# One four-byte inner product a unit in the expert stage, in place of three products of split operands

## The reference

```python
x = L0_attn_x                                   # (8, 512, 128): 4096 tokens of 128 channels
h = layernorm(x) * (1 + ca) + sa                # modulation rows from L0_c and L0_wmod
x = x + ga * attention(h, w_qkv, w_swiglu, w_out)
h = layernorm(x) * (1 + cb) + sb
# mixture of 16 experts, one expert a token, at most 320 tokens an expert
gate_logits = tokens @ gate_w.T
dispatch = einsum('sec,sd->ecd', sec_mask, tokens)     # (16, 320, 128)
hid = gelu(einsum('ecd,edf->ecf', dispatch, w1))       # w1: (16, 128, 512)
expert_out = einsum('ecf,efd->ecd', hid, w2)           # w2: (16, 512, 128)
out = einsum('sec,ecd->sd', combine_weights, expert_out)
return x + gb * out
```

## Time and profile before

| | |
|---|---|
| time, median of 3 runs | 205.05 us (204.35 to 205.32) |
| profiled execution, own time | 206.09 us |
| its span, first to last instruction | 204.2 us |
| PE busy | 191.0 us (94% of the span) |
| DVE busy | 148.2 us (73%) |
| ACT busy | 145.1 us (71%) |
| POOL busy | 123.0 us (60%) |
| clock granted to TensorE, mean | 0.985 of full |

### The profile page before, as it was taken

The page is one execution under the profiler, slowest core; times in us unless marked ns, Lnnn a source line. Parts: engine busy times, 40 slices in busy tenths (PEclk is TensorE's granted clock), DMA queues, the critical chain, the costliest instruction groups (busy, mean ns, idle before and its releaser), DMA issues.

```text
span 204.2 us, 4070 instructions
## 1 busy us (share of the span) xinstructions
PE 191.0 (94%) x1189; PEld 157.0 (77%) x1189; DVE 148.2 (73%) x467; ACT 145.1 (71%) x424; POOL 123.0 (60%) x154
## 2 busy tenths in 40 slices
PE   7998999999999999999968999999999999999960
PEld 4888778689888988777745568797888879787950
DVE  2658989999999999989972855284766756685530
ACT  4478999999999999888664835586584857553400
POOL 6232646274558888788776770505775845685774
PEclk9999999999999999999987999999999999999997
DMA  4999999979701332332499574996959575410110
GB/s 141 289 336 360 359 356 356 307 272 259 214 3 51 116 96 77 129 119 105 136 308 397 197 193 147 334 334 195 309 168 357 178 212 169 148 45 31 37 31 14
DMA packets 38597, 40.26 MB, mean 197 GB/s; under 512 B 2623, under 2 KB 32646, under 8 KB 38576
## 3 DMA queue, kind: packets, MB, share of 16 engines
q1 hardware_dynamic: 35248, 32.94, 51.4%
q0 software_dynamic: 3328, 7.07, 9.7%
HBM read 19.85 MB, written 19.94 MB: 195 GB/s over the span
## 4 chain that ended last, share of the span: by engine, by line
PE 78%; ACT 7%; POOL 4%; issue 4%; DVE 3%; DMA 2%; POOLq 1%; DVEq 0%; ACTq 0%
PE bank L1353 15%; PE bank L1339 12%; PE bank L1104 6%; PE bank L1122 4%; PE bank L1143 4%; PE bank L1148 4%; PE bank L1157 3%; POOL out_dram L568 3%; PE bank L1159 3%; PE bank L1115 3%; PE bank L1213 3%; PE bank L1174 2%; PE bank L1094 2%; ACT junk L599 2%; PE bank L1288 2%
## 5 line engine op out<-in xcount | busy, mean ns | idle before, releaser
L568 POOL DMA_INDIRECT out_dram<-x_all,rest x40 | 42.8, 1069 | 26.6 <-DVE x_all L1050 13.9
L531 POOL DMA_INDIRECT dispatched_rows<-rows,slot x32 | 32.5, 1016 | 10.1 <-issue 8.7
L748 ACT ACTIVATE HT<-bank 128x320 f32<-128x320 f32 x64 | 28.0, 438 | 10.6 <-PE bank L1339 10.2
L1353 PE MATMUL bank<-HT,w 128*128 128x320 f32 x112 | 32.4, 432 | 0.0
L1353 PEld LDWEIGHTS bank<-HT,w 128*128 128x128 f32 x112 | 20.7, 190 | 6.6
L1339 PE MATMUL bank<-xth,w1h 128*128 128x320 f32 x64 | 22.5, 352 | 0.0
L1339 PE MATMUL bank<-xtl,w1h 128*128 128x320 f32 x64 | 19.8, 309 | 0.0
L1339 PE MATMUL bank<-xth,w1l 128*128 128x320 f32 x64 | 19.8, 309 | 0.0
L1069 DVE COPY OT<-bank 128x320 f32<-128x320 f32 x14 | 6.9, 492 | 16.1 <-PE bank L1353 16.1
L599 ACT ACTIVATE junk<-bank 128x128 f32<-128x128 f32 x64 | 16.7, 306 | 2.3 <-PE bank L1104 2.3
L508 POOL TENSOR_TENSOR hsq<-hT 128x512 f32<-128x512 f32 x8 | 8.3, 1043 | 15.6 <-ACT hT L320 13.7
(11 more groups left out here) (178 smaller groups left out, 501.5 us busy)
## 6 DMA issues: line engine op xcount, KB each, us to landing
dispatched_rows<-blank SPq DMA_DIRECT2D x9, 965.0 KB, 12.8
w<-in_L_ffn_w_dram SPq DMA_DIRECT2D x16, 512.0 KB, 7.4
rest<-dispatched_rows SPq DMA_DIRECT2D x8, 645.0 KB, 5.5
hin<-dispatched_rows SPq DMA_DIRECT2D x7, 320.0 KB, 5.9
x_all<-in_L_attn_x_dram SPq DMA_DIRECT2D x8, 256.0 KB, 5.1
rows<-gb_row SPq DMA_DIRECT2D x8, 256.0 KB, 4.0
out_dram<-rows SPq DMA_DIRECT2D x8, 256.0 KB, 3.3
x_all<-dispatched_rows SPq DMA_DIRECT2D x1, 645.0 KB, 4.5
```

Of the source, the lines that this page charges most:

```text
L531: pool.indirect_dma_start(out=disp_d, out_offset=bass.IndirectOffsetOnAxis(ap=slot[:, b, j:j + 1], axis=0), in_=rows[:, b, j, :], in_offse ...
L568: pool.indirect_dma_start(out=out_d.rearrange("b t d -> (b t) d"), out_offset=bass.IndirectOffsetOnAxis(ap=rest[i % RING][:, n, C_TOK - D: ...
L748: act.activation(HT[e][:, f, :], ps_h[c % HB][:, 0:CAP], ACT.Gelu_apprx_tanh).then_inc(h_done, 1)
L1353: last = pe.matmul(ps_o[e], w2[i % RING][:, e, f, :], HT[e][:, f, :], start=(f == 0), stop=(f == NF - 1))
```

## The change

Each inner unit becomes one product of plain four-byte floats, with no split operands. The casts and subtractions of w1 and the subtractions of the tokens go; the tokens are copied once, into `xT` (ring of four). Of pair 0, DVE copies the second half (`last_half`). Unit f now takes block f of 128 hidden channels, so a block of w1 is used as it was loaded, and w2 is loaded with partition p holding rows p, 128 + p and so on: pieces of 512 bytes, in two transfers a pair. PE waits for the load of w1 itself, and SP reuses a buffer of w1 when the inner units of the pair that read it are done.

```diff
             def load_w1(i):
                 if i >= RING:
-                    sp.wait_ge(w1l_done, i - RING + 1)
+                    sp.wait_ge(h_ps, 2 * NF * (i - RING + 1))
...
-                sp.dma_start(w2[i % RING][:, :, :, :].rearrange("p e f d -> p e (f d)"),
-                             w2_d[2 * i:2 * i + 2, :, :].rearrange("e (p f) d -> p e (f d)", f=NF)
-                             ).then_inc(w2_in[i % RING], 16)
+                for e in range(2):
+                    sp.dma_start(w2[i % RING][:, e, :, :],
+                                 w2_d[2 * i + e, :, :].rearrange("(f p) d -> p f d", f=NF)
+                                 ).then_inc(w2_in[i % RING], 16)
...
-            def w1_high(i):
-                act.wait_ge(w1_in[i % RING], 16 * (i // RING + 1))
-                if i >= 2:
-                    act.wait_ge(h_ps, 2 * NF * (i - 1))
-                act.copy(w1h[i % 2][:, :, :, :], w1[i % RING][:, :, :].rearrange("p e (m f) -> p e f m", f=NF)
-                         ).then_inc(w1h_done, 1)
-
             def xt_high_halves():
                 act.wait_ge(head_ps, 1)
-                act.copy(xth[0][:, 0:CAP], ps_x0).then_inc(head_high, 1)
-                act.wait_ge(xt_ps, 1)
-                act.copy(xth[0][:, CAP:PS], ps_x1).then_inc(xth_done, 1)
+                act.copy(xT[0][:, 0:CAP], ps_x0).then_inc(head_done, 1)
...
-                act.copy(xth[i % 2][:, :], ps_xt).then_inc(xth_done, 1)
+                act.copy(xT[i % RING][:, :], ps_xt).then_inc(xt_done, 1)
...
-            w1_high(0)
-            w1_high(1)
...
-                if i + 2 < NPAIR:
-                    w1_high(i + 2)
...
-            def w1_low(i):
-                after(dve, w1h_done, i)
-                dve.tensor_tensor(w1l[i % 2][:, :, :, :],
-                                  w1[i % RING][:, :, :].rearrange("p e (m f) -> p e f m", f=NF),
-                                  w1h[i % 2][:, :, :, :].bitcast(f32), ALU.subtract).then_inc(w1l_done, 1)
...
+            def last_half():
+                dve.wait_ge(xt_ps, 1)
+                dve.tensor_copy(xT[0][:, CAP:PS], ps_x1).then_inc(xt_done, 1)
...
             def experts(i):
-                if 1 <= i < SPLIT:
-                    w1_low(i + 1)
...
-                if SPLIT <= i < LAST:
-                    w1_low(i + 1)
...
-                    if e == 0 and i < LAST:
-                        xt_low(i + 1)
...
-                after(pe, w1l_done, i)
+                pe.wait_ge(w1_in[i % RING], 16 * (i // RING + 1))
...
-                    for n, (w, x) in enumerate(((w1h, xth), (w1h, xtl), (w1l, xth))):
-                        last = pe.matmul(ps_h[c % HB][:, 0:CAP], w[i % 2][:, e, f, :],
-                                         x[i % 2][:, e * CAP:(e + 1) * CAP], start=(n == 0), stop=(n == 2))
-                    last.then_inc(h_ps, 1)
+                    pe.matmul(ps_h[c % HB][:, 0:CAP], w1[i % RING][:, e, f * P:(f + 1) * P],
+                              xT[i % RING][:, e * CAP:(e + 1) * CAP], start=True, stop=True).then_inc(h_ps, 1)
...
-                        pe.wait_ge(w2_in[i % RING], 16 * (i // RING + 1))
+                        pe.wait_ge(w2_in[i % RING], 32 * (i // RING + 1))
```

More of the change, by code:

```diff
@@ L147, in adaln_attention_moe @@
         w2 = [sb(f"w2_{n}", [P, 2, NF, D]) for n in range(2)]
-        w1h, w1l = [[sb(f"{name}{n}", [P, 2, NF, P], f32r) for n in range(2)]
-                    for name in ("w1h", "w1l")]
         RING = 4
-        hin, rest, HT, xth, xtl = [], [], [], [], []
+        hin, rest, HT, xT = [], [], [], []
         with ExitStack() as routed:
@@ L160, in adaln_attention_moe @@
             expert_buffers(HT, "HT", [P, NF, CAP], 2)
-            expert_buffers(xth, "xth", [P, PS], 2, f32r)
-            expert_buffers(xtl, "xtl", [P, PS], 2, f32r)
+            expert_buffers(xT, "xT", [P, PS], 4)
             expert_buffers(w1, "w1_", [P, 2, FF], RING)
@@ L243, in adaln_attention_moe @@
         ek_done, shift1_done = sem("ek_done"), sem("shift1_done")
-        w1h_done, w1l_done, xth_done = sem("w1h_done"), sem("w1l_done"), sem("xth_done")
         x1_first, x1_out = sem("x1_first"), sem("x1_out")
@@ L254, in adaln_attention_moe @@
         final_out = [sem(f"final_out{n}") for n in range(RING)]
-        head_in, head_ps, head_high, head_done = [
-            sem(n) for n in ("head_in", "head_ps", "head_high", "head_done")]
+        head_in, head_ps, head_done = [sem(n) for n in ("head_in", "head_ps", "head_done")]
         xt_ps, xt_done, h_ps, h_done, o_ps, o_done, y_ps, yw_done, fin_done = [
@@ L1069, in experts @@
                     dve.tensor_copy(OT[:, e * CAP:(e + 1) * CAP], ps_o[e]).then_inc(o_done, 1)
-                    if e == 0 and i < LAST:
-                        xt_low(i + 1)
-            w1_low(0)
             dve.wait_ge(x1_first, 16 * FIRST)
-            xt_low_halves()
-            w1_low(1)
+            last_half()
             for i in range(NPAIR):
```

## The result

The changed kernel takes 210.64 us (median of 4 runs, 209.26 to 212.08) against 205.19 us for the kernel before in the same comparison: a ratio of 1.026 (95% interval 1.017 to 1.035), slower by 5.45 us at the medians. The forecast was 210.4 us, in a range of 209.1 to 211.8.

The account below looks back on a forecast made before the run. PE's stream was taken to bound the expert stage through pair 6, then POOL's sends; 5.46 - 0.09 = +5.37 us, all else 0, on the 205.05 us median gives 210.4 us, range 209.1 to 211.8.

Parts of the forecast that it names:

- The price of a unit: Inner units on PE: three split products cost 440.0 ns, one four-byte product 537.5, so each unit gets 97.5 ns longer.
- PE's stream sets the time up to pair 6, and POOL's sends behind it: Expert stage: 56 units on an unbroken PE chain add 5.46 us; after pair 6's second product, POOL sends ten tiles back to back.
- The trap of the two records: Outer product on line 1353: 56 products leave 112 trace records, two each; eight records take 2.15 us, so one product costs 537.5 ns.
- rival 4: Inner units: the two records overlap, a lone unit costs 268.8 ns; -9.6 us, 195.4 us; chance 0.03.
- The head of pair 0: Start of pair 0: tokens reach PE after one copy without a subtraction, but PE fills that time with a filler product; 0.
- PE waited for none of the work on ACT and DVE: Expert stage: casts and subtractions that go were never waited for by PE, so removing them brings 0 on the path.
- the closing of the wait: Pair 6: PE's 0.09 us wait at 179.07 for DVE's weighing closes as units ahead take longer; -0.09 us.
- The 512-byte pieces: w2 loads: +0.45 us a pair on the DMA engines, +0.9 from 100 to 114 us, within 1.66 us of slack; 0.
- The freed work on ACT and DVE: ACT and DVE: eight casts of 2.06 us, eight subtractions of 2.03 and the tokens' subtractions go, bringing 0 on the path.
- Pair 7 under POOL's sends: End of the kernel: pair 7's eight units add 0.78 us on PE, covered by POOL's sends with 2.24 us of slack; 0.
- The later load of w1: SP's loads: w1 for pair 4 waits for pair 0's units, with more than 20 us of cover; 0.
- The rule beside the rows: Inner units: true FP32 takes four passes; at a split product's cost each, a unit takes 586.8 ns, sum +8.2 us.

Follow-up runs that it names:

- the first comparison: The changed kernel against the kernel before: 210.64 us against 205.19, ratio 1.026 (1.017 to 1.035).
- the second: The changed kernel timed and profiled again, no edit, against the kernel before: 210.05 us against 205.53, ratio 1.021 (1.017 to 1.026).
- the run that halves it: The kernel before with only the unit numbering and w2's 512-byte pieces changed, three split products kept: 205.54 us against 205.53, ratio 1.0016.

## Why the prediction was right

**The price of a unit** was the step that decided, and it held: 537.5 ns by the outer product's records, and the same by the new unit's own. Pairs 1 to 5 each got 0.79 us longer (8.92 to 9.71), against 0.78. That PE's stream sets the time up to pair 6, and POOL's sends behind it, held too.

**The near hit of the median is in part luck.** 210.64 lies 0.24 us from 210.4, but the medians are 5.45 us apart in the first comparison and 4.52 in the second, and the marks have +4.97. The second interval, up to +5.3, just leaves out the sum of +5.37. The profiled execution was put at a span of 209.6 and had 207.4: 1.77 us of that is its early start and 0.40 the terms below.

**The trap of the two records** was one. Whoever takes 268.8 ns for a product forecasts a kernel that is 9.6 us faster (rival 4); there are 128 records for 64 units.

**Two small terms were mis-sized.** The sum had +5.37; the marks have +4.97. The head of pair 0 was put at 0. It brought 0.28: pair 0 takes 9.16 us from the first mark against 8.66, only 0.50 more, not 0.78. In the kernel before, PE's first weight load stood 0.43 us waiting for DVE's subtraction of the tokens, so the first product began late with its filler already over; its 21 products to the first outer one took 3.34 us, where 146.7 ns each make 3.08. The load in the kernel before, and the piece of the chain behind it:

```profile
124.76 0.19 PEld L1339 LDWEIGHTS bank<-xth,w1h 128*128 128x128 f32 x1 [0.43 <-DVE xtl L1016]
```

```profile
124.76 3.34 PE bank L1339 x21
```

In the changed kernel that load starts ahead of the end of the filler (122.58 against 122.96):

```profile
122.58 1.48 PEld L1298 LDWEIGHTS bank<-xT,w 128*128 128x128 f32 x6
```

So the sentence that PE waited for none of the work on ACT and DVE was wrong in this one place. I had looked only at the idle time between products and not at the load in front of them. And in pair 6 the closing of the wait brought 0.20, not 0.09: the gap of 0.09 went, and the three transposes behind it take 0.41 us where they took 0.52. The third difference is the -0.08 us behind the second mark, which the second profile does not have. Together 5.46 - 0.28 - 0.20 - 0.08 = 4.90, within 0.1 of what the marks have.

**Edits costed at nothing.** The 512-byte pieces: shown to cost nothing, by the kernel with them alone. The freed work on ACT and DVE: shown to bring nothing on the path for w1's part, by the run that halves it and the run that puts it back; for the tokens' part only the 0.43 us at the head shows, and elsewhere the unbroken chain of PE argues it. Pair 7 under POOL's sends: shown, with 1.17 us more in pair 7 alone. The later load of w1: in the changed kernel's trace PE waits for no weight, and the load for pair 4 was issued at 130.00 us for products that begin at 161.25.

**The rule beside the rows.** The Trainium skill ("FP8 and Floating Point Precision", "TensorE Precision Notes") has four passes for true FP32. No run here shows the passes: the trace has two records a product. Four split products of 146.9 ns cost 587 ns in the run with four, and the four-byte product 537.5, a quarter of which is 134.4. The direction by that rule came out, slower; the price of a split product is not the price of a pass, and the row had to give it.

## What to carry to other kernels

Count a matmul's records against the instructions in the code before pricing it, and take its price from the pace of the chain, not from the duration of a record. Three cheap products can beat one expensive one, and work on engines that nobody waits for is free as long as that stays so; fewer instructions and idler engines say nothing until the chain names them. Before trusting that a faster engine gives all its time back, ask at what period the next one starts to matter: here it was 7.5 us a pair with the casts on ACT and 7.1 without, and two thirds of a gain of 16 us on paper were lost to ACT's order and POOL's sends.

## What the runs showed of the hardware

- In the kernel with only pieces and numbering changed, ACT's cast of w1 takes 1.05 us and DVE's subtraction 1.22, against 2.06 and 2.03: the same 128x1024 elements, read one after the other in place of every fourth (in the subtraction, one of its two inputs).
- DVE's cast of the same tile to fp32r, from SBUF to SBUF, takes 0.68 us (median of eight, in the kernel with one product of rounded operands):

```profile
L997 DVE CAST w1h<-w x8: 679/684/960, 117.3 to 170.1; 128x1024 fp32r<-128x1024 f32 x8
```

- Two executions of the changed kernel are 1.50 us apart at the first mark, most of it from the first 12 us; two filler products take 0.70 us in one and 1.22 in the other, while the granted clock of the windows from 6 to 9 and from 9 to 12 us reads 1.00 in both. The cause was not found.
